# Four small edits to a float32 layer stack: the first loads, one mask, paired transposes, the last block

## The reference

```python
# layer 0, conditional part: gated FFN with rank-16 adapters chosen per sequence
gate = x @ W_gate.T + 0.5 * (x @ A_gate[i].T) @ B_gate[i].T        # F = 1376
up   = x @ W_up.T   + 0.5 * (x @ A_up[i].T)   @ B_up[i].T
act  = silu(gate) * up
d    = act @ W_down.T + 0.5 * (act @ A_down[i].T) @ B_down[i].T
# layer 0, FFN part: one weight with eight weighted rank-16 adapters
x = x + d @ W.T + bias + sum_n 2 * w[n] * (d @ lora_A[n].T) @ lora_B[n].T
# layer 1, conditional part: one weight matrix per sequence
c = x @ W1.T + b + coeff[b] * (x @ (2 * mask[b] - 1))
# layer 1, FFN part: the 16 best of 64 rank-16 experts, with softmax gates
G = softmax over the top 16 of (c @ Wr.T)
x = x + 2 * sum_k G[k] * (c @ A[k].T) @ B[k].T
```

## Time and profile before

| | |
|---|---|
| median of 3 runs | 355.6 us |
| the profiled execution | 355.12 us |
| its span, first to last instruction | 353.4 us |
| TensorE busy | 349.5 us (99%), 1700 matmuls |
| VectorE busy | 199.6 us (56%) |
| ScalarE busy | 143.9 us (41%) |
| GpSimd busy | 78.5 us (22%) |
| read from HBM, written | 34.97 MB, 2.10 MB |

### The profile page before, as it was taken

The page is one execution under the profiler, slowest core; times in us unless marked ns, Lnnn a source line. Parts: engine busy times, 40 slices in busy tenths (PEclk is TensorE's granted clock), DMA queues, the critical chain, the costliest instruction groups (busy, mean ns, idle before and its releaser), DMA issues.

```text
span 353.4 us, 4654 instructions
## 1 busy us (share of the span) xinstructions
PE 349.5 (99%) x1700; PEld 295.3 (84%) x1700; DVE 199.6 (56%) x301; ACT 143.9 (41%) x196; POOL 78.5 (22%) x86
## 2 busy tenths in 40 slices
PE   8999999999999999999999999999999999999996
PEld 7899888888888888888888898888888888888886
DVE  4786655334533453685674565869888867511101
ACT  5666544422442243545464471466352443200100
POOL 2560657863440004000000000000051145002200
DMA  6961343232120053397219019010051022201011
GB/s 223 325 204 43 114 134 116 79 104 75 54 79 0 0 178 125 85 391 291 61 32 305 6 37 416 24 58 5 0 179 60 0 61 60 59 32 59 32 59 59
DMA packets 14803, 37.32 MB, mean 106 GB/s; under 512 B 2273, under 2 KB 4225, under 8 KB 13505
## 3 DMA queue, kind: packets, MB, share of 16 engines
q1 hardware_dynamic: 11920, 31.21, 25.4%
q0 software_dynamic: 2432, 5.57, 5.3%
q10 hardware_dynamic: 432, 0.30, 0.3%
HBM read 34.97 MB, written 2.10 MB: 105 GB/s over the span
## 4 chain that ended last, share of the span: by engine, by line
PE 99%; DVE 0%; issue 0%
PE ps L1153 29%; PE ps L1155 29%; PE ps L1154 29%; PE ps L1175 3%; PE ps L1305 3%; PE ps L1395 1%; PE ps L1382 1%; PE ps L1190 1%; PE ps L1183 1%; PE ps L1194 1%; PE ps L1198 1%; PE ps L1230 1%; PE ps L1404 0%; PE ps L1413 0%; DVE x L1146 0%
## 5 line engine op out<-in xcount | busy, mean ns | idle before, releaser
L1153 PE MATMUL ps<-x_hl,w_hl 128*128 128x512 f32 x144 | 56.1, 390 | 0.0
L1154 PE MATMUL ps<-x_hl,w_hl 128*128 128x512 f32 x144 | 56.1, 390 | 0.0
L1155 PE MATMUL ps<-x_hl,w_hl 128*128 128x512 f32 x144 | 56.0, 389 | 0.0
L460 POOL TENSOR_TENSOR am_hl<-am_raw,am_hl 128x512 fp32r<-128x512 f32 x8 | 11.0, 1387 | 137.7 <-ACT am_hl L477 137.7
L416 POOL DMA_INDIRECT b_raw<-b_gu,row_of x32 | 32.0, 999 | 30.2 <-DVE b_st L778 22.2
L798 DVE TENSOR_TENSOR glu<-glu,ps 128x512 f32<-128x512 f32 (+1 forms) x22 | 14.9, 683 | 39.3 <-ACT glu L509 27.3
L1155 PEld LDWEIGHTS ps<-x_hl,w_hl 128*128 128x128 f32 x144 | 27.0, 188 | 5.7
L509 ACT ACTIVATE glu<-ps 128x512 f32<-128x512 f32 (+1 forms) x22 | 12.8, 589 | 46.3 <-PE ps L1175 46.1
L1153 PEld LDWEIGHTS ps<-x_hl,w_hl 128*128 128x128 f32 x144 | 27.1, 188 | 5.3
L1154 PEld LDWEIGHTS ps<-x_hl,w_hl 128*128 128x128 f32 x144 | 27.1, 188 | 5.2
L1153 PE MATMUL ps<-act,wd_hl 128*128 128x512 f32 x80 | 31.1, 389 | 0.0
(11 more groups left out here) (151 smaller groups left out, 730.8 us busy)
## 6 DMA issues: line engine op xcount, KB each, us to landing
wc_raw<-mask_w SPq DMA_DIRECT2D x8, 1024.0 KB, 7.3
w_raw<-w_gu SPq DMA_DIRECT2D x8, 512.0 KB, 3.2
wd_raw<-w_dn SPq DMA_DIRECT2D x10, 256.0 KB, 2.7
w_raw<-w_t SPq DMA_DIRECT2D x2, 1024.0 KB, 7.1
x<-x_t SPq DMA_DIRECT2D x2, 1024.0 KB, 6.1
am_raw<-a_moe SPq DMA_DIRECT2D x8, 256.0 KB, 2.6
bm_raw<-b_moe SPq DMA_DIRECT2D x4, 512.0 KB, 4.4
x_raw<-x_t SPq DMA_DIRECT2D x7, 256.0 KB, 4.5
```

The source lines that it names most:

```text
L460: nc.gpsimd.tensor_tensor(am_hl[:, j % AM_SLOTS, 1], am_raw[:, j % 2], am_hl[:, j % AM_SLOTS, 0].bitcast(F32), ALU.subtract).then_inc(am_l ...
L1153: nc.tensor.matmul(out, w_high, m_high, start=start, stop=False)
L1154: nc.tensor.matmul(out, w_high, m_low, start=False, stop=False)
L1155: return nc.tensor.matmul(out, w_low, m_high, start=False, stop=stop)
```

## The change

Four edits.

1. The first load on ScalarE's queue is the gate half alone (64 KB); the up half is issued by SP between the two pairs of x's block 0. VectorE makes the gate's high and low part, ScalarE copies the up half after x's first pair. PE takes the gate's three products of pair 0, then the up half's, then pair 1. The warm-up matmuls read the framework's constant zeros, set before the kernel's first instruction, and wait for nothing.
2. t_mask(1) stands ahead of w_low(2, 0) on VectorE.
3. turn(b - 2) and turn(b - 1) stand together after cond(b) for even b; turn(6) and turn(7) stand together after the first part of experts(0). ScalarE's ct_high and VectorE's ct_low follow in twos, except that ct_low(4) stands before route_first8(0) and ct_low(5) behind c_bias(7).
4. In the last block (o = 3, s = 1) six of the eight rank tiles are summed with 512 columns in bank 7 and added to x2; the last two tiles (LAST_TILES) are done by pairs in banks 4 and 5 and added after that.

```diff
+                if h == 0:
+                    sp.dma_start(w_raw[0][:, 0, 1], w_gu[0, :, 0, 1]).then_inc(dma_up_first, 16)
             sp.dma_start(w_raw[1][:, 0], w_gu[1, :, 0]).then_inc(dma_w_first[1][0], 16)
...
-            act_e.dma_start(w_raw[0][:, 0], w_gu[0, :, 0]).then_inc(dma_w_first[0][0], 16)
+            act_e.dma_start(w_raw[0][:, 0, 0], w_gu[0, :, 0, 0]).then_inc(dma_w_first[0][0], 16)
...
                 copy(x_hl[:, 0, 0, pair], x_raw[:, 0, pair]).then_inc(x_hi if h else x_pair_hi, 1)
-            act_e.wait_ge(w_hi, 1)
+                if h == 0:
+                    act_e.wait_ge(dma_up_first, 16)
+                    copy(w_hl[0][:, 0, 0, 1], w_raw[0][:, 0, 1]).then_inc(w_hi, 1)
...
-                if b:
+                if b and b % 2 == 0:
+                    ct_high(b - 2)
                     ct_high(b - 1)
...
+            ct_high(BATCH - 2)
             ct_high(BATCH - 1)
...
             dve.wait_ge(dma_w_first[0][0], 16)
-            nc.vector.tensor_copy(w_hl[0][:, 0, 0:1], w_raw[0][:, 0:1]).then_inc(w_hi, 1)
+            nc.vector.tensor_copy(w_hl[0][:, 0, 0, 0], w_raw[0][:, 0, 0]).then_inc(gate_first_hi, 1)
+            dve.wait_ge(gate_first_hi, 1)
+            low(w_hl[0][:, 1, 0, 0], w_raw[0][:, 0, 0], w_hl[0][:, 0, 0, 0]).then_inc(gate_first_lo, 1)
...
             b_first_low(1)
+            t_mask(1)
             w_low(2, 0)
-            t_mask(1)
...
                 c_bias(b)
+                if b == 4:
+                    ct_low(2)
+                    ct_low(3)
                 if b + 2 < BATCH:
                     xs_low(b + 2)
...
-                if b:
-                    ct_low(b - 1)
+                if b == 2:
+                    ct_low(0)
+                    ct_low(1)
                 if 1 <= b < 5:
                     wc_low_half(5 + (b - 1) // 2, (b - 1) % 2)
                 if b == 6:
+                    ct_low(4)
                     route_first8(0)
+            ct_low(BATCH - 3)
+            ct_low(BATCH - 2)
             ct_low(BATCH - 1)
...
-            pe.wait_ge(warm_set, 1)
+            zeros = nc.const_aps.tensor(0.0, [P, P], F32)
             for _ in range(WARM_UP):
-                nc.tensor.matmul(ps[:, 7, 0:P], warm[:, 0:P], warm[:, 0:P], start=True, stop=True)
+                nc.tensor.matmul(ps[:, 7, 0:P], zeros, zeros, start=True, stop=True)
...
+            def first_pair(m):
+                pe.wait_ge(w_hi if m else gate_first_hi, 1)
+                pe.wait_ge(x_pair_hi, 1)
+                pair_of(0, m, 0, 0)
+                pe.wait_ge(w_lo if m else gate_first_lo, 1)
+                pair_of(0, m, 1, 0)
+                pe.wait_ge(x_pair_lo, 1)
+                pair_of(0, m, 0, 1)
+
+            def second_pair():
+                pe.wait_ge(x_hi, 1)
+                for m in range(2):
+                    pair_of(1, m, 0, 0)
+                    pair_of(1, m, 1, 0)
+                pe.wait_ge(x_lo, 1)
+                for m in range(2):
+                    pair_of(1, m, 0, 1)
...
-                turn(b - 1)
+                if b % 2 == 0:
+                    turn(b - 2)
+                    turn(b - 1)
                 if b == 6:
                     turn_scores(0)
             pe.wait_ge(c_done, BATCH - 1)
             experts(0, range(1))
+            turn(BATCH - 2)
             turn(BATCH - 1)
...
+            combine(KD - 1, 1, 1, range(LAST_TILES[0])).then_inc(o_ready, 1)
             for h in range(2):
-                if h == 1:
-                    pe.wait_ge(late_banks_free, 4 + 5)
-                combine(KD - 1, 1, 1, ps[:, 7 - 3 * h, 0:PAIR], slice(HALF + h * PAIR, HALF + h * PAIR + PAIR))
+                pe.wait_ge(late_banks_free, 4 + 4 + h + 1)
+                combine_pair(h)
```

More of the change, by code:

```diff
@@ L829, in _ @@
                 low(x_hl[:, 1, 0, pair], x_raw[:, 0, pair], x_hl[:, 0, 0, pair]).then_inc(x_lo if h else x_pair_lo, 1)
-                w_first_low(h, slice(0, 1), h + 1)
+                if h == 0:
+                    dve.wait_ge(w_hi, 1)
+                    low(w_hl[0][:, 1, 0, 1], w_raw[0][:, 0, 1], w_hl[0][:, 0, 0, 1]).then_inc(w_lo, 1)
+            w_first_low(1, slice(0, 1), 2)
             x_low(1, 0)
@@ L1136, in _ @@
             hg_low(2 * JT - 1)
-            for n in range(2 * KD - 1):
+            for n in range(2 * KD):
                 o, s = n // 2, n % 2
@@ L1144, in _ @@
                 pair = slice(HALF + h * PAIR, HALF + h * PAIR + PAIR)
-                dve.wait_ge(o_ready, 2 * KD + h)
-                nc.vector.tensor_tensor(x2[:, KD - 1, pair], ps[:, 7 - 3 * h, 0:PAIR], x2[:, KD - 1, pair], ALU.add)\
+                dve.wait_ge(o_ready, 2 * KD + h + 1)
+                dve.wait_ge(late_banks_free, 4 + 2 * KD)
+                nc.vector.tensor_tensor(x2[:, KD - 1, pair], ps[:, 4 + h, 0:PAIR], x2[:, KD - 1, pair], ALU.add)\
                     .then_inc(late_banks_free, 1)
@@ L1223, in adapt_first, with pair_of @@
                         adapt(b_st[1] if f else b_other, FIRST_BANK[n] + m, s)
-            def project_pair(h):
+            def pair_of(h, m, part_w, part_x):
                 pair = slice(h * PAIR, h * PAIR + PAIR)
-                def pass_of(part_w, part_x):
-                    for m in range(2):
-                        nc.tensor.matmul(ps[:, FIRST_BANK[0] + m, pair], w_hl[0][:, part_w, 0, m], x_hl[:, part_x, 0, pair],
-                                         start=h == part_w == part_x == 0, stop=False)
-                pe.wait_ge(w_hi, 1)
-                pe.wait_ge(x_hi if h else x_pair_hi, 1)
-                pass_of(0, 0)
-                pe.wait_ge(x_lo if h else x_pair_lo, 1)
-                pass_of(0, 1)
-                pe.wait_ge(w_lo, 1)
-                pass_of(1, 0)
-            for h in range(2):
-                project_pair(h)
+                nc.tensor.matmul(ps[:, FIRST_BANK[0] + m, pair], w_hl[0][:, part_w, 0, m], x_hl[:, part_x, 0, pair],
+                                 start=h == part_w == part_x == 0, stop=False)
+            def first_pair(m):
[14 more added lines that the diff above has]
+                    pair_of(1, m, 0, 1)
+            for m in range(2):
+                first_pair(m)
+            second_pair()
             project_first(1, 0)
@@ L1452, in _, with combine, combine_pair @@
                 experts(n)
-            def combine(o, u, s, bank, cols):
-                for j in range(JT):
-                    last = mm3(bank, bm_hl[:, u, 0, j], bm_hl[:, u, 1, j],
-                               hg[j // 2][:, j % 2, 0, cols], hg[j // 2][:, j % 2, 1, cols], j == 0, j == JT - 1)
+            def combine(o, u, s, tiles=range(JT)):
+                bank = ps[:, 4 + 2 * u + s]
+                for j in tiles:
+                    last = mm3(bank, bm_hl[:, u, 0, j], bm_hl[:, u, 1, j], hg[j // 2][:, j % 2, 0, halves(s)],
+                               hg[j // 2][:, j % 2, 1, halves(s)], j == 0, j == tiles[-1])
+                return last
+            def combine_pair(h):
+                cols = slice(HALF + h * PAIR, HALF + h * PAIR + PAIR)
+                for j in LAST_TILES:
+                    last = mm3(ps[:, 4 + h, 0:PAIR], bm_hl[:, 1, 0, j], bm_hl[:, 1, 1, j], hg[j // 2][:, j % 2, 0, cols],
+                               hg[j // 2][:, j % 2, 1, cols], j == LAST_TILES[0], j == LAST_TILES[-1])
                 last.then_inc(o_ready, 1)
```

12 lines of the change are left out of this document (7 added, 5 removed).

## The result

The changed kernel takes 357.69 us (median of six runs, 357.18 to 358.65), the one before 355.51 beside it (355.03 to 355.74). The ratio is 1.0065, 95% interval 1.0054 to 1.0076: **2.3 us slower**, 1.9 to 2.7. The forecast of 356.0 with its range up to 356.7 was wrong. The profiled execution took 357.28 us with a span of 355.6; before it was 355.12 and 353.4. So the two traces differ by 2.16 us, and that can be split by the starts of the same PE rows in both. One execution of all that follow, one of the pairs alone, ran at a granted clock of 0.658 and took 502.86 us; it is in none of the ratios, and every other one had 0.995 or more.

The account below looks back on a forecast made before the run. TensorE's matmul queue, busy 99% at full clock, was taken as the bound. Start +0.06, mask -0.20, middle +0.78 and last block -0.24 gave +0.40 us on the 355.6 median: 356.0 us, 8-in-10 range 354.9 to 356.7.

Parts of the forecast that it names:

- The start: First loads and warm-up, up to slot 1's first product: +0.06 us, range -0.35 to +0.46.
- rival A: Start: SP's extra slot delays slot 1's weights in full; total +0.81, 356.4 us; chance 0.17.
- rival C: Start: slot 1's weights land earlier, -0.35 for +0.06; total -0.01, 355.6 us; chance 0.15.
- everything SP issues afterwards: Start: SP's loads after slot 1's first weights, early adapter loads and x's second half included, move as well; no size given.
- t's mask: Before the adapter products: moving the mask up removes PE's stand; -0.20 us, range -0.26 to -0.15.
- Pair (0, 1): Middle, between cond(1) and cond(2): PE stands until xs_low(2) ends; +0.43 us, bounds +0.35 to +0.45.
- Pair (6, 7): Middle, after cond(7): turn(7) waits for ct_low(5), PE stands 0.49; +0.47 us, bounds 0 to 0.6.
- Rival B: Middle: the pairs' stands do not come and pairing works as meant; total -0.63, 355.0 us; chance 0.15.
- The last block: Kernel's end: 18 matmuls of 512 and 12 of 256 columns replace 48 of 256; -0.24 us, range -0.24 to -0.05.
- Rival D: Middle: clock falls around the second pair, one cond at the lower level; +2.72 + 0.40, 358.7 us; chance 0.03.
- the rule cited there: PE's clock: the Trainium skill says transposes do not count as busy for the clock gate like other matmuls; no size.
- no row is at the lower level: Whole kernel before: no PE row runs at 1.2 GHz, granted clock 1.00 over the span; no term given.

Follow-up runs that it names:

- the pairs alone: Kernel before with only the transposes by twos added: 356.70 us against 355.33, +1.0 us (0.5 to 1.4).
- the loads part: Kernel before with only the first loads, first splits and order of the first twelve products changed, old warm-up: 357.51 us against 355.33, +2.06 (1.4 to 2.7).
- the warm-up: Kernel before with only the warm-up changed (constant zeros, no wait): 355.35 us against 355.33, 0.0 (-0.4 to +0.4).
- mask and last block alone: Kernel before with only t's mask moved up and the new last block: 355.30 us against 355.33, -0.32 (-0.8 to +0.2).
- the first with GpSimd off the port: Kernel before plus pairs (turn(0), turn(1) single, ct_low(5) before routing), mask, last block, am_high(1) later on ScalarE: 355.79 us against 355.44, +0.35.
- the eight traces with unchanged loads: Traces of the kernel before, the warm-up alone, mask and last block, and five kernels with pairs but first loads as before; no single time.
- the two that mend them: Pairs with turn(0), turn(1) single and ct_low(5) ahead of routing: 356.31 us, +0.96; the same plus mask and last block: 356.12 us, +0.6.
- the last kernel of the middle: The first kernel with GpSimd off the port, plus ScalarE's second scores copy ahead of the third adapter tile's high part: 355.28 us, -0.35 against the kernel before.

## Why the prediction was wrong, by its own steps

- **The start** was taken at +0.06, bounds -0.35 to +0.46; the loads part measured +2.06 (1.4 to 2.7), the warm-up 0.0. This is the step that failed. Its rows were read rightly for the one landing it looked at: slot 1's weights came no later (5.41), so rival A (slower by that landing) did not happen. The condition of rival C, an earlier landing, came true, and its gain did not: that slot's first product is at 6.94 because of slow steps ahead of it, and not for want of its weights. The error is the sentence that named "everything SP issues afterwards" and gave it no price: a term put at nothing without a reason. I took what was true of the first landing for all of them. Every later tile of the first 17 us is used close behind its landing: before, the last tile's copies start at 11.77 and its product at 16.00, of which the copies and low parts need 3.52, so that 0.7 us are to spare. The stands came at the second half of W's tile 1 and at the last tile.
- **GpSimd's queue** was left out of the working altogether. The small inputs stood behind a load half as large as before and landed 1 us earlier (adapter loads at 5.45 for 6.45). An earlier start of other transfers was no term of my sum, and by the runs it is worth about 1.1 us.
- **t's mask** was -0.20; the stand is gone, 0.23 us from the projection to the adapter products. That stretch of the traces gives -0.15. In two of the five traces with this edit, mask and last block alone and the first with GpSimd off the port, a stand of 0.16 to 0.18 at the first adapter products takes it back.
- **Pair (0, 1)** was +0.43, and 0.43 is the stand in the trace.
- **Pair (6, 7)** was a stand of 0.49 and is one of 0.57. With T = 260.46, c_bias(7) starts at T + 0.26 (forecast 0.25), ct_low(5) at T + 0.86 (0.81), turn(7) at T + 1.69 (1.61): two small sizes, one mechanism. The middle gives +0.88 for +0.78, and the pairs alone +1.0 by the runs. Rival B, that they work as meant, is refuted.
- **The last block** was -0.24, and the trace has -0.24. Mask and last block together measured -0.32 for -0.44; the interval, -0.8 to +0.2, holds both the forecast and nothing.
- **Rival D**, the clock behind longer transposes, did not happen: the granted clock is 1.00 over the middle with the pairs as without them. No row shows the rule cited there at work. Its remark that no row is at the lower level does not hold, though no term hung on it. The warm-up's matmuls of 128 columns start some 0.22 us apart (14 of them from 1.18 to 4.23), transposes of 128 columns some 0.11 (four in 0.44). The column of the granted clock has 1.00 there, since the trace before has no entry for the clock. Timeline of PE before:

```profile
1.18 3.35 PE L1183 MATMUL ps<-warm 128*128 128x128 f32 x14 [1.18 <-DVE warm L818]
```

- Of the sum, +0.34 without the start, the traces have -0.15 + 0.88 - 0.24 = +0.49. The rest of the 2.16 us is the start. The terms other than the start were near by their mechanisms, and not by luck; the start alone puts the time outside the range.

## What to carry to other kernels

Where a kernel starts bound by its loads, price a changed issue list by every landing up to the point where PE has slack, and not by the first one. One issue of 0.47 us cost 0.85 (0.4 to 1.3) here, with the same bytes in the same order. Ask of every load that becomes shorter what it lets start earlier on other queues: about half of this loss went with adapter loads that nobody had touched. Find the stretch that varies before reading a cause from one pair of traces: the eight traces with unchanged loads differ by 0.85 us up to W's last tile, and the middle of those without pairs by 0.02. And before gathering small PE groups into larger ones, check what they were filling: the single transposes stood where PE would otherwise wait, and each repaired stand came back one step further on.

## What the runs showed of the hardware

- Delaying SP's issues by one place (0.47 us) cost +0.85 us (0.4 to 1.3) in the runs. In its trace the last tile's copy starts at 13.29, with unchanged loads at 11.77 to 13.04, and the DMA engines moved 264 GB/s between 5 and 9 us, with unchanged loads 292 to 327. The reason is open.
- VectorE's subtract of 128x256 with both inputs in SBUF takes 0.42 us alone, and 0.45, 0.88 and 1.55 us beside GpSimd's low parts, always ending 0.28 to 0.29 us after one of those. The scaling of the gates, of one SBUF tile by a column, was held as well (1.96 us, for 0.88 in the kernel ahead of it and 1.12 in the one before the change).
- The first twelve products run at one of two steps. In the changed kernel ten of them take from 4.54 to 6.94, 0.24 us each, most of them 0.213: the step that belongs to the granted clock 0.50 in the table of stretches above, though the PEclk column has 1.00 there. In the kernel before half of them step by 0.12 and all take 2.10 us.
- The slow step is not of this change alone. Every kernel with W's gate half first has it in its trace, for six to all of the twelve. But so have five of the eight traces with unchanged loads: the pairs alone, the two that mend them and the last kernel of the middle in nearly all steps, mask and last block in five. Where no later landing holds PE this costs time: in the trace of the pairs alone slot 1's first product comes at 6.93 for 6.33, PE does not stand behind it, and the first product with W's last tile comes at 16.61 for 16.00. In the changed kernel a later landing does hold PE, so none of its +1.66 is shown to be the clock's. The earlier warm-up is not the cause: alone, it leaves that product at 6.27, and with the loads part alone the steps are slow behind the old warm-up. The ratios of the runs cover many executions, and whether W's gate half first makes the slow step more frequent in them was not tried, nor what decides which level is granted.
